# Attention in pieces of 128 tokens instead of 64, with energies for half of the heads at a time

## What is computed

```python
q = silu(x @ Wq); k = silu(x @ Wk); v = x @ Wv             # 16 heads of 8
q = lrpe(q, theta); k = lrpe(k, theta)                     # [t*cos, t*sin]: 16 numbers a head
mask = tril(ones(n, n))
energy = einsum('bhnd,bhmd->bhnm', q, k) * mask            # no softmax
out = einsum('bhnm,bhmd->bhnd', energy, v)
out = layernorm((out @ Wo) * sigmoid(x @ G1 @ G2)) * gamma + beta
x = layernorm(x + out)
# mixture of 8 experts, 2 a token, capacity 1280, plus a shared FFN of width 1024
x = layernorm(x + shared(x) + routed(x))
```

## Time and profile before

| | us |
|---|---|
| median of three runs | 992.25 |
| the profiled execution | 985.05 |
| its span | 983.3 |
| TensorE busy | 915.9 (93%) |
| TensorE weight loads | 749.4 (76%) |
| VectorE busy | 566.2 (58%) |
| GpSimd busy | 381.1 (39%) |
| ScalarE busy | 303.1 (31%) |
| TensorE granted clock, mean | 0.952 |

### The profile page before, as it was taken

One profiled execution on the slowest core, in us unless ns is written; L12 is line 12 of the kernel. 1 busy time (PEld: TensorE's weight loads), 2 busy tenths in 40 slices (PEclk: granted clock), 3 DMA queues, 4 the chain that ended last, 5 costly groups with the idle time before them and its releaser, 6 DMA issues. The chain is left out here.

```text
span 983.3 us, 25364 instructions
## 1 busy us (share of the span) xinstructions
PE 915.9 (93%) x10102; PEld 749.4 (76%) x10102; DVE 566.2 (58%) x1851; ACT 303.1 (31%) x643; POOL 381.1 (39%) x362
## 2 busy tenths in 40 slices
PE   4998999999999999999999899758999999999996
PEld 3676787877778788777778666646999999988885
DVE  5465847566584756657575767743444444435652
ACT  6222323223231323223232212112333333235563
POOL 4004233140413224041322443354587887771220
PEclk8797999999999999999999978759999999999998
DMA  4413111020111102021121212103345554344331
GB/s 117 146 37 128 35 34 45 25 54 24 54 24 45 43 26 54 25 57 22 42 52 37 58 46 48 34 23 109 77 87 99 88 91 62 38 43 133 108 107 33
DMA packets 74197, 59.21 MB, mean 60 GB/s; under 512 B 10147, under 2 KB 64218, under 8 KB 74080
## 3 DMA queue, kind: packets, MB, share of 16 engines
q1 hardware_dynamic: 57312, 41.58, 15.3%
q0 software_dynamic: 16768, 16.01, 9.1%
HBM read 23.47 MB, written 28.89 MB: 53 GB/s over the span
## 5 line engine op out<-in xcount | busy, mean ns | idle before, releaser
L507 POOL DMA_INDIRECT dispatched_rows<-x,slot x128 | 126.2, 986 | 60.6 <-issue 39.5
L534 POOL DMA_INDIRECT summed_rows<-VP,goal_i x80 | 123.7, 1546 | 46.7 <-DVE VP L1030 24.0
L806 DVE TENSOR_TENSOR EM<-energy_banks,causal 128x512 f32<-128x512 f32 x128 | 87.6, 684 | 41.0 <-PE energy_banks L1152 41.0
L479 POOL TENSOR_TENSOR rr<-vq,minus_half 128x8 f32<-128x8 f32 x16 | 26.2, 1638 | 214.9 <-DVE vq L949 214.9
L1113 PE MATMUL bank<-xgT_hi,ws_hi 128*128 128x512 f32 x216 | 97.5, 451 | 10.6 <-DVE he L832 8.4
L832 DVE TENSOR_TENSOR he<-sf,bank 128x512 f32<-128x512 f32 x88 | 60.4, 686 | 81.2 <-PE bank L1115 63.2
L592 ACT ACTIVATE sf<-bank 128x512 f32<-128x512 f32 x88 | 52.6, 598 | 145.2 <-PE bank L1115 144.7
L1171 PEld LDWEIGHTS bank<-VP,Kt 64*128 64x128 f32 x448 | 61.4, 196 | 39.5 <-issue 37.4
L1227 PE MATMUL bank<-sd_s,he 128*128 128x128 f32 x704 | 84.2, 278 | 6.1 <-DVE he L832 6.1
L1115 PE MATMUL bank<-xgT_hi,ws_lo 128*128 128x512 f32 x216 | 87.5, 405 | 0.0
L1114 PE MATMUL bank<-xgT_lo,ws_hi 128*128 128x512 f32 x216 | 87.5, 405 | 0.0
(11 more groups left out here) (180 smaller groups left out, 1760.5 us busy)
## 6 DMA issues: line engine op xcount, KB each, us to landing
QM<-QT SPq DMA_DIRECT2D x256, 32.0 KB, 2.0
dispatched_rows<-empty POOLq DMA_DIRECT2D x8, 655.0 KB
QM<-dispatched_rows SPq DMA_DIRECT2D x8, 655.0 KB, 5.7
xin<-in_x SPq DMA_DIRECT2D x16, 256.0 KB, 3.0
QM<-summed_rows SPq DMA_DIRECT2D x16, 256.0 KB, 2.8
out_x<-QM SPq DMA_DIRECT2D x16, 256.0 KB, 2.3
summed_rows<-empty SPq DMA_DIRECT2D x11, 256.0 KB, 2.0
dispatched_rows<-x,slot POOLq DMA_INDIRECT x128
```

Source lines behind the costliest of these rows:

```text
L507: g.indirect_dma_start(out=xg_d, out_offset=bass.IndirectOffsetOnAxis(ap=slot[:, par, j:j + 1], axis=0), in_=x1[:, par, j % NC, :], in_off ...
L534: g.indirect_dma_start(out=sum_d, out_offset=bass.IndirectOffsetOnAxis(ap=goal_i[:, par, t:t + 1], axis=0), in_=ye[:, par, t, :], in_offse ...
L806: v.tensor_tensor(EM[:, c % 2, i], EB2[:, i].rearrange("p (h n) -> p h n", h=8), causal[:].unsqueeze(1).broadcast_to([P, 8, T]), ALU.mult) ...
```

## The change

Pieces are 128 tokens. There are three states a block (NS = 3) in place of seven, each from 128 tokens. `energies(c, i)` is called twice a chunk, once for each half i of the heads: two products of 64 channels by 128 keys by 4 heads x 128 queries, one for each row half of the array, each into its own bank of `EB2`. So the two banks hold one half of the heads of a chunk, and the second call must wait until VectorE has masked what the first one wrote. `attend` runs once a chunk, with 128 queries in each product, in `part(c, 1)`; `state` runs in `part(c, 0)`. On VectorE `mask(b, par, c, i)` now does two maskings of 128x512 and one `SM` copy a chunk. `QM` has one buffer, so the DMAs for the next block wait for this block's energies of chunk 1 (first half of the tokens) and chunk 3 (second half). The triangle `causal` grows from 64 to 128 columns, one of two clearings of `QM` at the start goes, and in stage 3 the tile `x1t` lies at another place of `QM`.

```diff
-T = 64
-NS = S // T - 1
+NS = NC - 1
...
-        QM = sb("QM", [P, 2, 2, 2, 2, 4, P])
+        QM = sb("QM", [P, 2, 2, 2, 4, P])
...
-        EM = sb("EM", [P, 2, 2, 8, T])
+        EM = sb("EM", [P, 2, 2, 2, 4, P])
...
@@ SyncE @@
                     need(sp, v_qk, 4 * b + 6)
-                    need(sp, pe_E, 8 * b)
                     for g2 in (0, 1):
+                        need(sp, pe_E, 16 * b + 8 * g2 + 8)
                         for h in range(8):
                             rows = slice(16 * h, 16 * h + 16)
-                            sp.dma_start(QM[rows, 1 - par, g2, :, :, h % 4].rearrange("p t c n -> p (t c) n"),
+                            sp.dma_start(QM[rows, g2, :, :, h % 4].rearrange("p t c n -> p (t c) n"),
                                          QT[rows, 1 - par, g2].rearrange("p t (c n) -> p (t c) n", c=2)).then_inc(g_qm[g2], 16)
@@ ScalarE @@
-                    clear(flat(QM)[:, 32 * P:64 * P], 32 * P).then_inc(z_qm, 1)
@@ VectorE: mask @@
-                    need(dve, pe_E, 8 * b + 2 * c + i + 1)
-                    need(dve, pe_av, 4 * b + c - 1)
-                    v.tensor_tensor(EM[:, c % 2, i], EB2[:, i].rearrange("p (h n) -> p h n", h=8),
-                                    causal[:].unsqueeze(1).broadcast_to([P, 8, T]), ALU.mult).then_inc(v_mask, 1)
-                    k = 2 * c + i
-                    if k < NS:
-                        need(dve, pe_S, NS * b + k + 1)
-                        need(dve, pe_av, 4 * (b - 1) + (k + 1) // 2 + 1)
-                        v.tensor_tensor(SM[:, k], SBK[:, 0:128], headmask[:].rearrange("p t n -> p (t n)"),
+                    for r in (0, 1):
+                        need(dve, pe_E, 16 * b + 4 * c + 2 * i + r + 1)
+                        need(dve, pe_av, 4 * b + c - 1)
+                        v.tensor_tensor(EM[:, c % 2, i, r], EB2[:, r].rearrange("p (h n) -> p h n", h=4),
+                                        causal[:].unsqueeze(1).broadcast_to([P, 4, P]), ALU.mult).then_inc(v_mask, 1)
+                    if i == 0 and c < NS:
+                        need(dve, pe_S, NS * b + c + 1)
+                        need(dve, pe_av, 4 * (b - 1) + c + 2)
+                        v.tensor_tensor(SM[:, c], SBK[:, 0:128], headmask[:].rearrange("p t n -> p (t n)"),
                                         ALU.mult).then_inc(v_S, 1)
@@ TensorE @@
+                def energies(c, i):
...
+                    need(pe, v_mask, 16 * b + 4 * c + 2 * i)
+                    for r in (0, 1):
+                        rows = slice(64 * r, 64 * r + 64)
+                        t.matmul(EB2[:, r], KT[rows, par, i, P * c:P * (c + 1)],
+                                 QM[rows, c // 2, i, c % 2], start=True, stop=True).then_inc(pe_E, 1)
...
+                    need(pe, v_S, NS * b + c)
                     for half in (0, 1):
-                        ins = t.matmul(SBK[:, T * half:T * half + T], Kt[tok, par, c, P * half:P * half + P],
-                                       v_rows(par, c, half, tok), start=(k == 0 and half == 0), stop=True,
+                        ins = t.matmul(SBK[:, 64 * half:64 * half + 64], Kt[:, par, c, P * half:P * half + P],
+                                       v_rows(par, c, half), start=(c == 0 and half == 0), stop=True,
...
-                def attend(b, par, c, s):
+                def attend(b, par, c):
...
+                    need(pe, a_out, 4 * b + c)
+                    need(pe, v_S, NS * b + c)
+                    need(pe, v_mask, 16 * b + 4 * c + 4)
+                    tok = slice(P * c, P * (c + 1))
                     for half in (0, 1):
-                        if k > 0:
...
+                        if c > 0:
+                            t.matmul(OB[64 * half:64 * half + 64, tok], SM[:, c - 1, 64 * half:64 * half + 64],
+                                     QT[:, par, c // 2, half, P * (c % 2):P * (c % 2) + P], start=True, stop=False)
                     for i in range(4):
                         for j in range(4):
                             h = 4 * j + i
-                            ins = t.matmul(OB[32 * j:32 * j + 32, tok], VP[keys, par, c, 32 * h:32 * h + 32],
-                                           EM[keys, c % 2, h % 8 // 4, h // 8 * 4 + h % 4], start=(k == 0 and i == 0), stop=(i == 3))
-                    ins.then_inc((pe_av0, pe_av)[s], 1)
+                            ins = t.matmul(OB[32 * j:32 * j + 32, tok], VP[:, par, c, 32 * h:32 * h + 32],
+                                           EM[:, c % 2, h // 8, h % 8 // 4, h % 4], start=(c == 0 and i == 0), stop=(i == 3))
+                    ins.then_inc(pe_av, 1)
...
                 def part(c, s):
 
                     if core:
+                        energies(c, s)
                         if s == 0:
-                            energies(c)
-                        state(c, s)
-                    if c > 0 and core:
-                        attend(b, par, c - 1, s)
-                    elif c == 0 and back:
-                        attend(b - 1, 1 - par, 3, s)
+                            state(c)
+                    if s == 1 and c > 0 and core:
+                        attend(b, par, c - 1)
+                    elif s == 1 and c == 0 and back:
+                        attend(b - 1, 1 - par, 3)
```

More of the change, by code:

```diff
@@ L441, in _ @@
                    allow_small_or_imprecise_dtypes=True).then_inc(c_pool, 1)
[L442 to L446 removed]
+            gp.wait_ge(c_pool, 13)
+            g.affine_select(out=causal[:], in_=causal[:], compare_op=ALU.is_ge, fill=0.0, base=0,
+                            pattern=[[1, P]], channel_multiplier=-1).then_inc(c_pool, 1)
+            gp.wait_ge(c_pool, 14)
             g.affine_select(out=before_f, in_=before_f, compare_op=ALU.is_gt, fill=0.0, base=0,
```

67 lines of the change are left out of this document (17 added, 50 removed).

## The result

| | before | after |
|---|---|---|
| median of the runs, us | 993.25 (992.24 to 995.18, 4 runs) | 1021.77 (1019.18 to 1022.86, 4 runs) |
| ratio after to before | | 1.0281, 95% interval 1.0253 to 1.0309 |
| profiled execution, us | 985.05 | 1020.83 |
| its span and mean granted clock | 983.3, 0.952 | 1019.1, 0.962 |
| TensorE busy, VectorE busy, us | | 918.2, 625.9 |

The change costs 28.5 us, or 2.8%. The forecast was 1028, range 1010 to 1050, slower at 0.93: the sign and the range hold, the number is 6 us high. The lower clock is not the reason for the loss, since the mean clock of the slower kernel is the higher one.

What follows compares the result with a forecast made beforehand. TensorE bounds FFN blocks, with VectorE's tail almost level; elsewhere TensorE waits for VectorE. Terms 10.3 + 4.1 + 6.7 + 5.8 + 6.2 + 2.5 = 35.6 us on a median of 992.25 gave 1028, range 1010 to 1050.

Steps and rivals of the forecast that it cites:

- the same distance: Last step: the median of the runs again lies 7.2 us above the profiled execution, 992.25 + 35.6 = 1027.9 us.
- Columns set TensorE's price: TensorE's attention calls: columns, not number of instructions, set the time; energies 1.02 us, values 1.01, state copy times queries 0.37.
- Rival 1: TensorE in `attend`: instructions, not columns, set the price; 109 us less in sixteen blocks, near 932 us; chance 0.04.
- Rival 2: New energies on TensorE: the two 64x128 halves don't run together, each call 1.87 us, near 1135 us; chance 0.04.
- Rival 3: Values on TensorE: weight loads sharing rows don't overlap with running products; +55 us, near 1083 us; chance 0.04.
- TensorE's sum: TensorE's attention calls per block: 14.74 us before, 14.69 after; with fewer shape changes its work falls by 0.25 us.
- The new wait: Second energies wait for VectorE's maskings: about 1.2 us at chunk 3 in FFN blocks, at each chunk in plain blocks.
- the forecast's own five steps: FFN blocks, down product to VectorE's tail: parts of chunks 0 to 2 change by +0.97, -0.81, +0.60, -1.07, +0.97; together +0.66 us.
- clock term: Granted clock over the kernel: longer, more frequent waits bring more low-clock stretches; +2.5 us, between -2 and +15.
- `QM` at nothing: DMAs into the single `QM` buffer: they wait for chunks 1 and 3 but are wanted later, so cost nothing.
- Rival 4: Placing hides more: VectorE has no part in the FFN blocks' path, only other blocks lose; 5 to 18 us; chance 0.08.
- Rival 5: Whole kernel: no measurable change, TensorE's sum being 2 us a block too high; chance 0.03.

Runs made afterwards that it cites:

- experiment 10: Changed kernel with 256 columns instead of 512 in each product of energies, half of the heads' energies left out: 1004.0 us, ratio 1.0127.
- experiment 8: Changed kernel with the first maskings of chunk 3 ahead of VectorE's layer-norm work, second ones moved up in blocks without FFN: 1015.29 us, ratio 1.0241.
- experiment 6: Kernel before with the small copy of the expert numbers (L966) moved up, out of GpSimd's way, run without the gaps: 995.0 us, ratio 1.0038.
- experiment 11: Changed kernel, unchanged, run once more: 1022.94 us, ratio 1.0290.
- later groups: Second and third groups of timed runs, without the gaps; the kernel before had medians of 991.4 us (17 runs) and 993.4 us (23 runs).
- experiment 2: Kernel before with one buffer of `QM` instead of two, filled as after the change: 1090.14 us, ratio 0.9977.
- experiment 4: Kernel before with one `QM` buffer and every masking done twice, the first into a scratch tile, without the gaps: 1020.53 us, ratio 1.0270.
- experiment 9: Changed kernel with each masking over 128x256 instead of 128x512, so its output is not the layer's: 996.7 us, ratio 1.0046.
- experiment 1: Kernel before, unchanged, run again in an hour when TensorE stood still in each FFN block: 1093.02 us, ratio 1.0007.
- experiments 5: Kernel before with the small copy of the expert numbers (L966) moved up, run while the gaps were present: 1091.45 us, ratio 1.0002.
- first group: First of three groups of timed runs, each beside the kernel before, which had a median of 1092.8 us here (29 runs).

## Why the prediction was right, and by how much it was off

The block periods of the two profiles, against the terms of the sum, in us:

| stretch | forecast | measured |
|---|---|---|
| blocks 0 and 1 | +6.2 | +1.7 and +4.6 |
| blocks 2 to 11 (FFN) | +10.3 | +13.5 (block 2 -1.1, the others +14.6) |
| block 12 | +4.1 | +3.1 |
| block 13 | +3.35 | +3.3 |
| block 14 | +3.35 | +0.8 |
| block 15 to the first product of the experts | +5.8 | +7.0 |
| from there to the end | 0 | +1.8 |
| clock | +2.5 | within the rows above |
| between the two profiled executions | +35.6 | +35.8 |
| to the medians | the same distance, 7.2 | +28.5 in the end |

And FFN blocks (block 7, or block 5 in experiment 10) cut in two: from the down product, which waits for the eighth hidden of the block before, to the first energies of chunk 3, and from these to the start of the next eighth hidden. The 0.73 us that are left in each row are the hidden itself and the signal.

| kernel | to the energies of chunk 3 | to the eighth hidden | period |
|---|---|---|---|
| before | 31.16 | 11.59 | 43.48 |
| before, maskings doubled (4) | 31.15 | 12.35 | 44.23 |
| changed | 32.17 | 12.16 | 45.06 |
| changed, first maskings of chunk 3 early (8) | 32.17 | 12.15 | 45.05 |
| changed, maskings of half the size (9) | 32.10 | 11.62 | 44.46 |
| changed, energies of 256 columns (10) | 30.04 | 12.14 | 42.91 |

In these rows the first part moves only with TensorE's work and the second only with VectorE's. So of the 1.57 us that the change costs such a block, 1.0 is TensorE's own work and 0.57 VectorE's.

- **Columns set TensorE's price: right.** Energies 1.06 (forecast 1.02), values 1.01, state copy 0.37, state 0.47 (0.46). Rivals 1, 2 and 3 fall with these rows; each would have changed a call by 0.4 us or more.
- **TensorE's sum: mis-sized.** Forecast -0.25 us a block, measured +0.48 busy in block 7. With the measured durations the calls give 8 x 1.06 + 4 x 1.01 + 3 x 0.37 + 3 x 0.47 = 15.04 for 14.74, +0.30; and behind each state the first FFN product takes 0.31 to the next in place of 0.23, +0.24: the state has a new shape behind it after all, which the forecast had at nothing.
- **The new wait: right in place and size** (1.12 for 1.2, at chunk 3 alone in FFN blocks; at each chunk in the others). But experiment 8 shows that in FFN blocks it is a place where time is spent and not its cause: without it the block is as long.
- **FFN blocks: the term mis-sized, +1.03 for +1.6.** Up to the energies of chunk 3 the growth was 1.01 (32.17 for 31.16) where the forecast had 0.66, by the dearer energies and states: with the measured durations, and 0.08 more behind each state, the forecast's own five steps add up to 1.0. In the tail it was 0.57 (12.16 for 11.59, to the start of the eighth hidden) where it had 0.37. VectorE's stall at the copy did shrink, as forecast, from 1.05 us to 0.2 (now at L959), and swallowed most of the delay. Block 2 went the other way, by 1.1, and the clock explains it: it ran at 0.85 before and at 0.92 after, and in the kernel of experiment 6, also at 0.92, it took 42.62, so that at one clock it is 1.2 us longer after the change, not shorter. Block 2 before, then after:

```profile
74.75:119.66 44.91, 41.12 (x486) 30.40 (x486) 29.61 (x87) 12.73 (x28) 14.28 (x13) 0.85 0.25 82
80.89:124.72 43.83, 38.58 (x293) 24.81 (x294) 33.82 (x93) 12.73 (x28) 14.33 (x13) 0.92 0.25 83
```

- **Blocks without FFN: right** for 12 and 13, by luck in part: in the second profile of the changed kernel (experiment 11) both ran at 0.93 of the clock and took 2.4 and 2.3 us more. Block 14 was forecast from a block at 0.80 of the clock; after the change it ran at 0.91, so the clock gave 2.5 us back there where I had added 2.5. **The sign of the clock term was wrong.** Errors of opposite sign (FFN +3.2 and the ends of the stages +3, clock and block 14 -5) made the sum look better than its parts.
- **The step that failed is the last one, "with the same distance".** The profiled execution of before lay 7.2 us under its median, that of after 0.9 under its own. In the later groups the kernel before ran between 985.91 and 1001.46 us (40 runs), with a span of 988.0 at a mean clock of 0.947 and of 994.1 at 0.942: its profile was a run at the fast edge. The distance was a property of that one execution. This alone is the 6 us by which the forecast was high. Where it lay, the profile of experiment 6 suggests (994.83 us, near the median of before, with FFN blocks of 43.41): most of it is block 15, up to the first product of the experts. First the kernel before, then experiment 6, then the changed kernel:

```profile
603.58:681.05 77.47, 56.45 (x628) 43.81 (x628) 40.43 (x197) 8.88 (x20) 43.25 (x42) 0.74 0.14 40
605.36:689.43 84.07, 65.85 (x628) 51.04 (x628) 40.58 (x196) 8.88 (x20) 43.38 (x42) 0.63 0.13 37
630.56:715.06 84.50, 55.33 (x402) 37.48 (x399) 45.05 (x199) 9.15 (x22) 42.51 (x42) 0.79 0.13 37
```

  The same instructions of TensorE take 6.6 us longer at 0.63 of the clock than at 0.74, and against that the changed kernel loses 0.4 us there in place of 7.0. No profile of the unchanged kernel near its median, without the gaps, was taken.
- **`QM` at nothing: right** (experiment 2). **Rival 4** (only blocks without FFN lose) is wrong by the FFN blocks' 13.5 us; its 5 to 18 us did not fit the forecast's own terms for the other blocks either, which add up to 22.8. **Rival 5** falls with the 28.5 us.
- **Whose loss it is.** VectorE's load alone can cost this much: experiment 4 gives 27 us without the new shapes, experiment 9 takes 23 to 25 back while keeping them. But it isn't all of the loss. After experiment 9 the ten FFN blocks still take 11 us more than in the kernel of experiment 6 (444.4 for 433.3), which is TensorE's 1.0 a block, and that hardly shows in the total because the others take less than there (blocks 12 to 14 92.7 us at 0.98 of the clock for 94.9 at 0.89, block 15 to the experts 79.6 at 0.79 for 84.1 at 0.63). So in the FFN blocks about two thirds of the loss are TensorE's own work and one third VectorE's; in the others TensorE waits for maskings.

Open: what the gaps of experiment 1 are; why the low clock comes in one block of the two; and what the change costs with the clock the same in both kernels.

## What to carry to other kernels

Changes of shape that nearly cancel on the engine that bounds the kernel (here +0.48 us a block) can still cost: the path changes from one engine to the other within the block, so what counts is how much of the work comes ahead of that point (here +1.0 us) and how much the other engine has behind it (+0.57). Count too what a larger piece does to the elementwise work (here, whole 128x128 triangles in place of halved ones, eight maskings more a block); where two engines are almost level part of any such load comes out. A wait seen in the trace isn't a cause until a run without it is shorter; moving it (experiment 8) or moving its victim (experiments 5 and 6) only passed it on. And before a change is added to a profiled execution, ask how far that execution lies from the median and whether the clock of its stretches explains that.

## What the runs showed of the hardware that was not expected

- In the first group TensorE stood still for reasons that no record shows ("issue"), 26.3 us before L1195 alone in 35 times, all but one in the small products behind the first down product of an FFN block, with the clock at 0.50 behind it: 1092.8 us for 992. Whether the number of instructions matters there was not settled.
- The wait of VectorE for GpSimd's addition (L484) went from the copy to the next operation with two SBUF inputs: copy 1.22 us for 0.17, pair of TENSOR_TENSOR 1.34 for 0.29. Beside GpSimd's instruction before it (L479) such an operation took no longer (0.19).
- The kernel of experiment 6 spent block 15, up to its last values, at half clock (0.50, 34.1 us); the profiled execution of the kernel before was at 0.81 there (25.0 us), and the changed kernel between 0.82 and 0.93 (30.6 to 32.5 us in three profiles, one of them with the copy early).
- Taking 3.4 us a block off TensorE (experiment 10) gave 2.15 in blocks at full clock and in others, at 0.76 to 0.79 of it, took 2 to 3 us more.
